# Router logits taken from the output projection's products instead of from the transposed normalised rows, in a one-layer decoder with mixture of experts

## What is computed

```python
x = layernorm(x + self_attention(x))             # causal, per-head layer norm on q and k
x = layernorm(x + cross_attention(x, ctx))       # rotary q and k, biases on q, k, v and the output
logits = x @ router_w.T                          # [4096, 8]
top, idx = top_k(logits, 2); probs = softmax(top)
x = layernorm(x + sum_k probs_k * expert_idx_k(x))   # expert: gelu(x @ w1.T + b1) @ w2.T + b2
```

## Time and profile before

| | |
|---|---|
| median of 3 runs | 1096.5 us (1096.5 to 1098.51) |
| the profiled execution | 1108.46 us |
| its span, first to last instruction | 1106.7 us |
| TensorE matmul (PE) | 1029.5 us, 93% |
| VectorE (DVE) | 720.3 us, 65% |
| ScalarE (ACT) | 602.2 us, 54% |
| GpSimd (POOL) | 290.7 us, 26% |
| chain of waits | PE 77%, DVE 7%, issue 7%, ACT 5% |

### The profile page before, as it was taken

The page is one execution under the profiler, slowest core; times in us unless marked ns, Lnnn a source line. Parts: engine busy times, 40 slices in busy tenths (PEclk is TensorE's granted clock), DMA queues, the critical chain, the costliest instruction groups (busy, mean ns, idle before and its releaser), DMA issues.

```text
span 1106.7 us, 29609 instructions
## 1 busy us (share of the span) xinstructions
PE 1029.5 (93%) x10991; PEld 766.0 (69%) x10991; DVE 720.3 (65%) x1642; ACT 602.2 (54%) x1032; POOL 290.7 (26%) x399
## 2 busy tenths in 40 slices
PE   8899999999999999999999999987887999999994
PEld 5556666666667766666666666654587899999983
DVE  5656666666667877767787868777254544456766
ACT  4666776777666655666556666554534222222335
POOL 1144232223223310000222121314244532222221
PEclk9999999999999999999999999999899999999997
DMA  4237544654562000100010010001355877788884
GB/s 155 86 125 246 172 142 158 206 163 133 177 200 40 21 12 12 50 12 12 22 42 32 32 37 27 23 20 43 118 163 167 251 223 219 212 285 294 270 275 158
DMA packets 96379, 139.30 MB, mean 126 GB/s; under 512 B 11408, under 2 KB 69136, under 8 KB 95984
## 3 DMA queue, kind: packets, MB, share of 16 engines
q1 hardware_dynamic: 89616, 114.99, 33.1%
q0 software_dynamic: 6624, 22.42, 5.5%
HBM read 76.56 MB, written 60.29 MB: 124 GB/s over the span
## 4 chain that ended last, share of the span: by engine, by line
PE 77%; DVE 7%; issue 7%; ACT 5%; another core or an unknown queue 2%; DVEq 2%; DMA 1%; ACTq 0%
PE PS L671 12%; PE PS L692 11%; PE PS L905 7%; PE PS L921 7%; PE PS L641 6%; PE PS L745 5%; PE PS L749 5%; PE PS L763 4%; PE PS L816 4%; PE PS L790 3%; PE PS L648 2%; PE PS L779 2%; ACT pT L1049 2%; PE PS L644 2%
## 5 line engine op out<-in xcount | busy, mean ns | idle before, releaser
L1347 DVE TENSOR_REDUCE part<-PS 128x6 f32<-128x768 f32 (+1 forms) x256 | 270.1, 1087 | 118.3 <-PE PS L648 84.8
L1049 ACT ACTIVATE pT<-PS 128x768 f32<-128x768 f32 (+1 forms) x256 | 220.9, 915 | 107.8 <-PE PS L671 95.7
L1922 POOL TENSOR_SCALAR_AFFINE_SELECT pT<-pT 128x512 f32<-128x512 f32 x128 | 84.5, 661 | 274.6 <-ACT pT L1049 270.9
L671 PE MATMUL PS<-big 32*128 32x256 f32 (+1 forms) x2048 | 133.9, 374 | 23.7 <-issue 13.8
L671 PEld LDWEIGHTS PS<-big 32*128 32x128 f32 x2048 | 96.1, 184 | 66.1 <-issue 62.8
L905 PEld LDWEIGHTS PS<-x1T,big 128*128 128x128 f32 x1136 | 137.3, 192 | 6.4 <-ACT x1T L1174 2.6
L905 PE MATMUL PS<-x1T,big 128*128 128x128 f32 x1136 | 138.8, 275 | 1.1 <-ACT x1T L1174 1.1
L692 PE MATMUL PS<-pT,vaug 128*32 128x256 f32 (+1 forms) x2048 | 126.0, 363 | 8.1 <-ACT big L1100 2.4
L2012 POOL DMA_INDIRECT p_dram<-sq,rowid x71 | 69.4, 978 | 167.1 <-DVE rowid L1682 124.9
L1060 ACT ACTIVATE oT<-PS 128x256 f32<-128x256 f32 x128 | 49.2, 384 | 106.8 <-PE PS L692 104.9
L692 PEld LDWEIGHTS PS<-pT,vaug 128*32 128x32 f32 x2048 | 58.6, 110 | 60.0 <-issue 35.2
(11 more groups left out here) (218 smaller groups left out, 1679.5 us busy)
## 6 DMA issues: line engine op xcount, KB each, us to landing
big<-w SPq DMA_DIRECT2D x71, 512.0 KB
xs_dram<-zrow SPq DMA_DIRECT2D x24, 1496.0 KB, 9.5
vaug<-xs_dram SPq DMA_DIRECT2D x71, 136.0 KB
xin<-xT SPq DMA_DIRECT2D x16, 256.0 KB, 2.9
xb<-x SPq DMA_DIRECT2D x16, 256.0 KB, 11.2
w2s<-w POOLq DMA_DIRECT2D x1, 4096.0 KB, 14.3
xin<-ctxT SPq DMA_DIRECT2D x16, 256.0 KB, 2.7
rows_all<-p_dram SPq DMA_DIRECT2D x8, 512.0 KB
```

The source lines that it names most:

```text
L671: ins = pe.matmul(o, keys, a[r0:r1, 0, g, q0:T], start=True, stop=True)
L1049: act.activation(pT[:, k % 2, 2 * half:2 * half + 2, 0:wide], src, ACT.Exp).then_inc((exp_a, exp_b)[half], 1)
L1347: dve.tensor_reduce(dst, src, AX.X, ALU.max, negate=True).then_inc((max_a, max_b)[half], 1)
L1922: pool.affine_select(d, d, [[0, 2], [0, 2], [1, P]], ALU.is_ge, 0.0, base=0, channel_multiplier=-1).then_inc(masked, 1)
```

## The change

Since the logits are linear, they can be had before the layer norm. With y the residual sum, r the reciprocal root and m the mean of a row, the logits are (y - m) r W, and y is onT times Wo plus the bias plus x1. So:

- The router's weights are centred once (their mean over the features is subtracted), multiplied with Wo and laid behind it: wx_o has 264 columns instead of 256. The same is done for the output bias (cb). These one-time products are four jobs `fold_router(0..3)` in quarters 20 to 23 with `take_fold` on VectorE: 4 transposes, 4 matmul instructions, 2 transposes, 12 matmul instructions, each job with its place in the ring.
- `rate_x1(n)`, with r = 0 behind `project_qk(n, 0)`, multiplies x1T with the centred router weights (8 instructions, job x1z, VectorE adds cb and keeps it in `raw`). It stands at q = 4n, where `rate` stood at 4n + 25.
- The output projection of a crossed block no longer fits one bank (528 columns), so it is two jobs wo0 and wo1, one for each row tile. `residual` takes four VectorE instructions (two of 128x256, two of 128x8) instead of one.
- `turn_x2`, `drain_x2T`, `rate` and their jobs x2T and logits are gone. `take_logits` multiplies `raw` with the reciprocal roots, and stands before `moments_of`.
- Handing over: ScalarE's gelu stands before `seed_roots` and `exp_gap`; VectorE's `tile_steps` stands before `take_roots` with r = 3; GpSimd's `combine_weights` is one quarter later from quarter 140 on.
- At the end the first of the four last groups is normalised on VectorE (`scale_group`, four instructions of 128x256 with one source) between `refine_roots` and `measure` of the next, instead of on ScalarE.

```diff
@@ ring_places @@
         if r == 0:
-            place("qk0", block_at(q, QK_AT))
-            n = block_at(q, LN_AT)
-            place("x2T", n, n is not None and crossed(n))
+            n = block_at(q, QK_AT)
+            place("qk0", n)
+            place("x1z", n, n is not None and crossed(n))
         elif r == 1:
-            n = block_at(q, LOGITS_AT)
-            place("logits", n, n is not None and crossed(n))
...
             place("x1T", n, n is not None and crossed(n))
-            place("wo", block_at(q, PROJECT_AT))
+            n = block_at(q, PROJECT_AT)
+            for part in wo_jobs(n):
+                place(part, n)
             place("rank", routed_at(q, RANK_AT))
+        if 0 <= q - FOLD_AT < FOLDS:
+            place("fold", q - FOLD_AT)
...
@@ TensorE @@
+                if crossed(n):
+                    for t in range(NT):
+                        job = (wo_jobs(n)[t], n)
+                        await_room(pe, job)
+                        for c in range(KC):
+                            ins = pe.matmul(ring_slot(job)[:, 0:E + NE], onT[:, c, t * P:(t + 1) * P],
+                                            wx_o[:, c, :], start=(c == 0), stop=(c == KC - 1))
+                        ins.then_inc(filled_by(job), 1)
+                    return
...
                 if r == 0:
                     project_qk(block_at(q, QK_AT), 0)
-                    turn_x2(block_at(q, LN_AT))
+                    rate_x1(block_at(q, QK_AT))
                 elif r == 1:
-                    rate(block_at(q, LOGITS_AT))
...
+                elif 0 <= q - FOLD_AT < FOLDS:
+                    fold_router(q - FOLD_AT)
...
@@ ScalarE @@
                 turn_out(q - TILES_AT)
+                gelu(q - TILES_AT - 1)
                 if r == 3 and q >= TILES_AT:
                     seed_roots(block_at(q, CHAIN_AT), block_at(q, ROOT_AT))
                     exp_gap(routed_at(q, RANK_AT))
-                gelu(q - TILES_AT - 1)
                 if r == 0:
                     drain_qk(block_at(q, QK_AT), 0)
-                    drain_x2T(block_at(q, LN_AT))
...
             def normalise_group(group):
                 act.wait_ge(norm_ready, group + 1)
+                act.wait_ge(normed, group)
...
-            normalise_group(ENDING[0])
...
@@ VectorE @@
+                if crossed(n):
+                    await_drained(dve, ("x1z", n))
+                    for t in range(NT):
+                        job = (wo_jobs(n)[t], n)
+                        await_filled(dve, job)
+                        dve.tensor_tensor(y[:, n % 2, t], ring_slot(job)[:, 0:E], xb[:, n % 2, t], ALU.add)
+                        dve.tensor_tensor(raw[:, n % 8, t], ring_slot(job)[:, E:E + NE], raw[:, n % 8, t], ALU.add
+                                          ).then_inc(drained_by(job), 1)
+                    return
...
+                dve.tensor_tensor(lg[:, j:j + NT, :], raw[:, n % 8], bc(chain[:, 1, 2:4], NE), ALU.mult
+                                  ).then_inc(router_link, 1)
...
                 elif r == 1:
                     maxima(group_at(q, SCORE_AT), 0)
                     maxima(group_at(q, SCORE_AT), 1)
+                    choose_second(routed_at(q, SECOND_AT))
+                    take_logits(block_at(q, LOGITS_AT))
                     moments_of(block_at(q, MOMENTS_AT))
-                    choose_second(routed_at(q, SECOND_AT))
                     tile_steps(q)
-                    take_logits(block_at(q, LOGITS_AT))
...
                     combine(block_at(q, MAXT_AT - 1))
+                    tile_steps(q)
                     take_roots(block_at(q, CHAIN_AT), block_at(q, ROOT_AT))
                     lay_out(block_at(q, LAY_AT))
-                    tile_steps(q)
                     residual(block_at(q, PROJECT_AT))
...
             refine_roots(ENDING[0])
+            scale_group(ENDING[0])
             measure(ENDING[2])
...
```

132 lines of the change are left out of this document (97 added, 35 removed).

## The result

The changed kernel takes **1117.76 us** (median of 4 runs, 1115.29 to 1119.68); the kernel before, timed beside it, 1097.51 (1096.5 to 1099.04). The ratio is **1.0176** [1.0153, 1.0199], the square brackets being its 95% interval: 20.2 us slower. The forecast said slower, by 10.5 us at the median; 1117.76 is just inside the upper end of its range, 1118, and the size is off by a factor of two.

What follows compares the result with a forecast made beforehand. TensorE, busy 93% of the span, was taken to bound the kernel. Terms 3.5 + 3.1 - 2.6 + 0.9 + 13.0 + 0 - 8 + 0.9 = +10.8 gave 1119.3 us profiled, 1107 median, range 1095 to 1118.

Steps and rivals of the forecast that it cites:

- terms 1 and 2: One-time folding jobs, +3.5 us; product x1z added in six blocks, quarters 64 to 84, with nothing removed yet, +3.1 us.
- term 5: Cross attention: wo1 waits for ScalarE's drain of x1T, 11 times 1.3 us, less 1.3 for rank jobs: +13.0 us.
- Term 4: Output projection with 264 columns for 256, 0.06 us in each of 16 blocks: +0.9 us.
- Term 3: Quarters 88 to 124, ten blocks: logits' product moved and transposes gone, four blocks waiting for VectorE's rotation: -2.6 us.
- term 7: Hand-over to the expert tiles: a 4.92 us wait near block 31 and x2T's other work go: -8 us (-4 to -14).
- Term 6: Quarters 128 to 139: removed x2T and product lay where TensorE waits for the exponentials: 0 us (to -4).
- rival of the clock: Each of the 11 new waits brings a lower-clock stretch, 13.8 us more, 1121 us in all; chance 0.08.
- Term 8: The end: four scalings on VectorE make the last normalisation start later: +0.9 us (0 to +1.5).

Runs made afterwards that it cites:

- after: The changed kernel, nothing altered: its profiled execution from the session of the result, 1117.25 us.
- e4: The changed kernel again, unaltered: 1140.59 us, 1.0232 of the kernel before.
- e0: The kernel before again, unaltered, for a second profile: 1111.97 us.
- e1: The changed kernel with job x1T placed behind wo0 and wo1 in the ring: 1128.95 us, 1.0146 of the kernel before.
- e16: The changed kernel with VectorE's second choice of the router behind the rotation of qk1, except its first instruction: 1136.90 us, 1.0231 of the kernel before.
- e12: The changed kernel a third time, unaltered: 1120.42 us, 1.0185 of the kernel before.
- e5: The changed kernel with VectorE's residual ahead of take_roots from quarter 140 on: 1136.70 us, 1.0207 of the kernel before.
- e2: The changed kernel with the three reorderings of the hand-over undone: 1135.55 us, 1.0198 of the kernel before.
- e7: The kernel before with only the three reorderings of the hand-over added: 1115.13 us, 1.0023 of the kernel before.
- e19: The changed kernel with x1T behind wo0 and wo1, residual ahead of take_roots from quarter 140, useless TensorE work in quarters 136 and 137: 1101.75 us, 1.0034 of before.
- e8: The changed kernel with useless TensorE work in quarters 136 and 137: 1116.72 us, 1.0171 of the kernel before.
- e18: The changed kernel with x1T behind wo0 and wo1 and residual ahead of take_roots from quarter 140 on: 1104.22 us, 1.0053 of the kernel before.

## Why the prediction was right and wrong

Split at two blocks, predicted against measured (after against the first trace of before, which has stalls; in brackets e4 against e0, both with stalls, the fairer pair):

- *Block 0 to 16, terms 1 and 2*: +6.1 (3.5, and five of the six blocks), measured +5.9 (+5.9). **Right.** The folding shows as +2.9 by block 2, the added product as +3.0.
- *Block 16 to 27, terms 3, 4, 5 and the sixth block*: +11.6, measured +8.3 (+10.9). **Right, a little high.** Of term 5 the place, the count and the mechanism are shown by e1. It was put at 13.0; removing the waits gives 12.0 us over these blocks with stalls and 9.9 without. The single wait is 1.07 us by its row, 1.39 start to start, where I had 1.3. Term 4: an instruction of 264 columns takes 386 ns at the median (one of 256: 379), 0.06 for the eight, as worked out. Term 3 had the wait for VectorE's rotation, but for four blocks and not six; e16 shows that moving the choice only moves the wait.
- *Behind block 27, terms 6 to 8*: -6.9, measured (+11.2). **Wrong**, and of the pair with stalls it is nearly the whole of the miss: 18 of 19 us. By the stages of the table, e4 against e0: block 27 to 30 +4.0; tile 3 to 4 +7.2; tile 8 to 9 -6.9; tile 9 to 15 +6.1, the longer stalls; the end +1.3; the rest, -0.5. For a session without stalls the kernel before has no trace, so the 20.2 us of the result can't be split in the same way; of them 5.9 stand ahead of block 16 and some 8 to 11 in blocks 16 to 27, so 3 to 6 us slower are left for what was forecast as 6.9 faster. Without stalls tile 9 to 15 is 26.8 and 27.0 in the changed kernel (after, e12), and tile 15 to 20 has the wait for p_dram in its place: 23.8 and 25.4 against 20.4 in the kernel before.

**The step that failed is term 7**, "-8 (-4 to -14)". The 4.92 us at 838.45 did go (-6.0 and -6.9 at tile 8 to 9), but over tiles 0 to 20, where term 7 stands, the changed kernel takes 7.1 us more with stalls (104.4 against 97.3) and not 8 less. I asked "what is late next" only of that wait. The same edit that adds wo0 and wo1 to the ring changes the bank of every job behind them, and I followed this to x1T and not on to the rank job of quarter 143, where VectorE's drain is behind a table load: +6 to +7, as much as that gain (e5: the wait goes, and tile 3 to 4 falls from 12.9 to 7.2). Term 5 says "In four of these quarters there is a rank job" and takes their wait as saved; in the hand-over it is a new one. The other transposes and products of x2T, -1.3 and -2.8, are there: tiles 1 to 3 and 4 to 8 take 1.5 and 3.1 less than before (6.7 and 15.7). VectorE's wait for p_dram takes most of that back: without stalls tile 0 to 20 takes 95.1 us (99.5 in e12), before 95.8 with its stalls, so -0.7 at best for -8. The three reorderings, to which I ascribed part of the gain, have no share in it: without them tile 8 to 9 is as short (e2), and in the kernel before they gain nothing (e7).

**Term 6**, "0 (to -4)", has probably the wrong sign. I saw that TensorE waits for the exponentials in those quarters and took work out of a wait to be worth nothing. Putting such work back gave 2.5 us (e19) and 3.7 (e8), with intervals that overlap, and a high clock more often; the stretch from block 27 to 30 is 4.0 us longer in e4 than in e0. How much of the 20.2 us it is stays open, since after and the first trace of before have the same 0.86 ahead of block 30. The rival of the clock put the loss at the 11 new waits; there the granted clock is 1.00 (window from 430), so that rival is out. The Trainium skill (TensorE: Matmul & The Clock Gate, "A second HAM failure mode: psum-queue depth-cycling") says of another kernel that micro-idles between groups of matmuls make the clock go up and down. The 11 waits of 1.07 us don't bear that out here; in the trace after, where it is low, the waits just ahead were 2.43, 1.27 and 3.40 us (at 785.45, 791.46 and 821.73).

Term 8 was 0.9 and is 1.3 to 1.7; its own figures, four scalings of 0.286 us, come to 1.1. Of GpSimd's `combine_weights` the prediction says "costs nothing while that order holds". Whether it owns VectorE's wait of 4.6 us stays open.

**The ratio.** I carried the sum from an execution of 1108.46 us to a median of 1096.5. Between them are 12 us. That trace has 20.9 us of waits of ScalarE without a releaser, and the changed kernel's traces without them are of faster sessions; so the 12 us are probably stalls, though no trace of a 1097 us execution shows it. One of the stalls, [4.40 <-remote] at 830.82 in the earlier trace rows, stood within the very chain that term 7 shortened. What such a chain costs where there is no stall could not be read from it.

What is left when both waits are gone is 5.6 us (e18), 3.2 with the work of e19. The traces show costs that stay: the folding (2.9), the product added ahead of block 16 (3.0), the end (1.3 to 1.7) and the wait for p_dram. Against them stand the transposes that the change saves; how the rest adds up was not worked out. No version tried beats the kernel before.

## What to carry to other kernels

When a job is added to a ring of two banks, write down for every job behind it which bank it now gets and who drains that bank, in each stage, and not only for the nearest pair. Before taking work out of an engine's wait, look what the granted clock does in that stretch: here work put back into such waits seems to have been worth 2 to 4 us. And compare the profiled execution with the median before reading a stage closely: when they differ by 1%, find the waits that make up the difference, and don't price an edit by a row that stands behind one.

## What was not expected of the hardware

The same program takes 1098 us in three sessions and 1112 to 1113 in three others, steadily within each. In the traces of the slower sessions, and in the first trace of the kernel before, ScalarE has waits that no releaser explains, at much the same places in each. Waits of e0, and its timeline at one of those of L1049:

```profile
ACT x1T L1174 <- remote: 12.8, 3, 4.5
ACT pT L1049 <- remote: 10.2, 4, 2.6
```

```profile
566.02 0.96 POOL L1985 DMA_INDIRECT xs_dram<-rows_all,posi  x1 [0.30 <-ACT oT L1060]
566.45 1.89 DVE L1504 TENSOR_TENSOR sel<-lg,top 128x32 f32<-128x32 f32 x1
...
568.30 1.94 ACT L1049 ACTIVATE pT<-PS 128x1024 f32<-128x1024 f32 x2 [2.57 <-remote]
568.37 0.19 DVE L1506 TENSOR_TENSOR sel<-sel,rev 128x32 f32<-128x32 f32 x1
```

VectorE's step of 0.19 us takes 1.89 and ScalarE stands for 2.57; both go on at 568.3. In the cross attention this comes every 53 us, at every second block, and GpSimd's indirect DMAs of the scatter, which run then, are just ahead. That they cause the stall is not shown: the changed kernel has the same DMAs in the faster sessions and no such stall beside them. What makes the difference between the sessions was not found; one chip was in a session of either kind (e0, e18). For the changed kernel the traces show the stalls in the slower sessions alone (34 us in e4, none in after and e12). For the kernel before only traces with stalls exist.

A change can make these stalls dearer without adding any: with three of them, blocks 16 to 27 take 3.4 us longer than without in the changed kernel (298.7 against 295.3), and 1.3 with x1T moved (286.7 against 285.4). A likely reason is that TensorE waits for ScalarE's drain in the former, so that a stall of ScalarE goes straight into the wait; it was not tested apart.
